# A fast-feedforward tree stage on one core: the leaf mask product over 128 zero-padded rows instead of 16

## What is computed

```python
def _fff(x, node_w, node_b, w1, b1, w2, b2):
    xf = x.reshape(-1, D)
    cur = jnp.zeros((N,), jnp.int32)
    for _ in range(DEPTH):
        score = jnp.einsum('nd,nd->n', xf, node_w[cur]) + node_b[cur]
        cur = 2 * cur + 1 + (score >= 0).astype(jnp.int32)
    sel = jax.nn.one_hot(cur - N_NODES, N_LEAVES, dtype=xf.dtype)
    hidden_all = jax.nn.relu(jnp.einsum('nd,ldh->lnh', xf, w1) + b1[:, None, :])
    hidden = hidden_all * sel.T[:, :, None]
    out = jnp.einsum('lnh,lho->no', hidden, w2) + sel @ b2
    return out.reshape(Bx, Sx, D)
```

## Time and profile before

| | us |
|---|---|
| median of three runs | 1661.69 |
| lowest, highest | 1656.72, 1661.87 |
| the profiled execution, its own time | 1658.01 |
| its span, first to last instruction | 1656.2 |
| TensorE matmul busy in the span | 1468.4 (89%) |
| VectorE, ScalarE, GpSimd busy | 994.2, 652.8, 640.2 |

### The profile page before, as it was taken

The page is one execution under the profiler, slowest core; times in us unless marked ns, Lnnn a source line. Parts: engine busy times, 40 slices in busy tenths (PEclk is TensorE's granted clock), DMA queues, the critical chain, the costliest instruction groups (busy, mean ns, idle before and its releaser), DMA issues. The chain is left out here.

```text
span 1656.2 us, 29794 instructions
## 1 busy us (share of the span) xinstructions
PE 1468.4 (89%) x11472; PEld 1147.0 (69%) x11472; DVE 994.2 (60%) x1896; ACT 652.8 (39%) x1266; POOL 640.2 (39%) x558
## 2 busy tenths in 40 slices
PE   6988877765993899999999999999999994789998
PEld 3645645444893688888888888888888873456676
DVE  4999954476237456666666665666566643464444
ACT  1444432131201455555555555555455431322322
POOL 0000000001002557877767877677876531311100
PEclk9777788867996999999999999999899965899999
DMA  9479700800322666676676675676674531220000
GB/s 357 145 281 323 264 0 1 296 1 0 104 101 88 172 167 153 163 195 164 153 162 155 159 187 150 157 166 148 164 188 101 112 66 51 80 102 0 1 1 26
DMA packets 109296, 219.61 MB, mean 133 GB/s; under 512 B 10871, under 2 KB 83095, under 8 KB 108391
## 3 DMA queue, kind: packets, MB, share of 16 engines
q1 hardware_dynamic: 109163, 217.80, 47.0%
HBM read 132.51 MB, written 6.40 MB: 84 GB/s over the span
## 5 line engine op out<-in xcount | busy, mean ns | idle before, releaser
L1905 DVE TENSOR_REDUCE d_top<-psum 128x1 f32<-128x400 f32 (+2 forms) x512 | 270.4, 570 | 97.6 <-PE psum L1549 90.4
L1449 POOL TENSOR_TENSOR d_ring<-d_ring 128x512 f32<-128x512 f32 x224 | 289.8, 1294 | 77.0 <-ACT d_ring L1734 59.4
L1734 ACT ACTIVATE d_ring<-psum 128x512 f32<-128x512 f32 (+1 forms) x416 | 229.3, 595 | 206.2 <-PE psum L1567 187.2
L1567 PEld LDWEIGHTS psum<-d_queries,d_stack 100*128 100x128 f32 (+1 forms) x1664 | 214.3, 198 | 36.3 <-issue 33.7
L1567 PE MATMUL psum<-d_queries,d_stack 100*128 100x128 f32 (+1 forms) x1664 | 235.4, 286 | 1.2 <-DVE d_queries L1920 0.9
L1549 PE MATMUL psum<-d_stack,d_queries 96*128 96x400 f32 (+1 forms) x512 | 171.6, 393 | 13.4 <-DVE d_top L1905 10.6
L1379 POOL TENSOR_TENSOR d_rowsT<-d_raw,d_rowsT 128x768 fp32r<-128x768 f32 (+2 forms) x62 | 117.9, 1903 | 154.0 <-ACT d_rowsT L1705 154.0
L1534 PE MATMUL psum<-d_wv,d_rowsT 128*128 128x256 f32 (+1 forms) x1248 | 170.4, 286 | 0.0
L1526 PE MATMUL psum<-d_rowsT,d_wk 128*128 128x384 f32 (+2 forms) x768 | 160.3, 358 | 3.6 <-POOL d_rowsT L1379 1.9
L1534 PEld LDWEIGHTS psum<-d_wv,d_rowsT 128*128 128x128 f32 (+1 forms) x1248 | 161.9, 187 | 0.5 <-issue 0.5
L973 POOL TENSOR_TENSOR c_partL<-moe_in,c_partH 128x256 fp32r<-128x256 f32 x8 | 5.5, 730 | 388.5 <-ACT c_partH L1061 388.5
(11 more groups left out here) (393 smaller groups left out, 2303.0 us busy)
## 6 DMA issues: line engine op xcount, KB each, us to landing
d_stack<-d_stage SPq DMA_DIRECT2D x384, 200.2 KB, 4.2
a_cR<-ctx_rows_dram SPq DMA_DIRECT2D x16, 1664.0 KB, 9.5
a_cT<-ctxT_dram SPq DMA_DIRECT2D x16, 1601.0 KB, 14.5
moe_w<-moe_w_dram SPq DMA_DIRECT2D x16, 1024.0 KB, 11.3
d_rowstd<-row_stds_dram SPq DMA_DIRECT2D x16, 801.0 KB, 5.7
d_raw<-ctxT_dram SPq DMA_DIRECT2D x32, 384.0 KB, 5.7
d_raw<-ctxT_dram SPq DMA_DIRECT2D x16, 512.0 KB, 6.3
d_queries<-queries_dram SPq DMA_DIRECT2D x96, 64.0 KB, 2.0
```

The source lines that it names most:

```text
L1449: pool.tensor_tensor(sums[:, 0, m, :], first, ring[:, slot_of(u, m, c), :], ALU.add)\
L1567: last = pe.matmul(ps[0:w, S_BANK + (m + c) % 2, j * P:(j + 1) * P], stack[0:STACKED, m, j, c * P:c * P + w], queries[0:STACKED, m, j, :], ...
L1734: act.activation(ring[0:w, slot_of(u, m, c), :], ps[0:w, S_BANK + (m + c) % 2, :], ACT.Exp)\
L1905: dve.tensor_reduce(top[:, m, v:v + 1], ps[:, M_BANK + v % 2, 0:min(w, S - s0)], X, ALU.max)\
```

## The change

`member`, `leaf_raw` and `leafT` get 128 partitions. `member` becomes three operands, one for each tree, each 128 x 1024 with only that tree's 16 rows other than zero. The matmul of line 2233 so contracts over all 128 partitions for every tree. `path` gets 128 columns, so that `leafT` gets 128 rows, those outside the leaves being zero. On GpSimd a clear of the larger `leaf_raw` (128 x 3072 words) comes second, right after that of `b2_raw`, and SyncE's wait before the six small loads is for both. ScalarE rounds `member` in three instructions of 128 x 1024 where there was one of 80 x 1024, and does so after the last of the four exponentials and before the square roots. The bias matmuls of 16 rows (lines 2244 and 2264) stay.

```diff
-        path = core.tensor(ctx, "f_path", [TREES * NNODE, LEAVES], BF16)
+        path = core.tensor(ctx, "f_path", [TREES * NNODE, P], BF16)
-        leaf_raw = core.tensor(ctx, "f_leaf_raw", [LEAVES, HC * P])
+        leaf_raw = core.tensor(ctx, "f_leaf_raw", [P, TREES, HC * P])
-        leafT = core.tensor(ctx, "f_leafT", [LEAVES, N], F32R)
-        member = core.tensor(ctx, "f_member", [LEAVES, HC, P], F32R)
+        leafT = core.tensor(ctx, "f_leafT", [P, N], F32R)
+        member = core.tensor(ctx, "f_member", [P, TREES, HC * P], F32R)
...
-            sp.wait_ge(sig("f_b2_clear"), 1)
+            sp.wait_ge(sig("f_clear"), 2)
...
-                sp.dma_start(leaf_raw[32 * j:32 * j + rows, :], drams["pg"][0:rows, NN + TREES * D:NN + TREES * D + HC * P])\
+                sp.dma_start(leaf_raw[32 * j:32 * j + rows, j, :], drams["pg"][0:rows, NN + TREES * D:NN + TREES * D + HC * P])\
                   .then_inc(sig("f_leaf_in"), 16)
...
-            pool.memset(b2_raw[:, :], 0.0).then_inc(sig("f_b2_clear"), 1)
+            pool.memset(b2_raw[:, :], 0.0).then_inc(sig("f_clear"), 1)
+            pool.memset(leaf_raw[:, :, :], 0.0).then_inc(sig("f_clear"), 1)
...
-                pe.matmul(ps[0:LEAVES, 2 + c, :], path[:, :], right[:, cols_of(c)], start=True, stop=True)\
+                pe.matmul(ps[:, 2 + c, :], path[:, :], right[:, cols_of(c)], start=True, stop=True)\
                   .then_inc(sig("f_leafT_ps"), 1)
             pe.wait_ge(sig("f_xL"), 2 * KD)
-            pe.wait_ge(sig("f_member"), 1)
+            pe.wait_ge(sig("f_member"), TREES)
...
-                pe.matmul(ps[:, n % 4, :], member[leaves(j), h, :], leafT[leaves(j), cols_of(c)], start=False, stop=True)\
+                pe.matmul(ps[:, n % 4, :], member[:, j, h * P:(h + 1) * P], leafT[:, cols_of(c)], start=False, stop=True)\
                   .then_inc(sig("f_hid_ps"), 1)
...
-            act.activation(member[:, :, :], leaf_raw[:, :].rearrange("p (c n) -> p c n", c=HC), ACT.Copy)\
-               .then_inc(sig("f_member"), 1)
             act.activation(b2[0][:, :], b2_raw[:, :], ACT.Copy).then_inc(sig("f_b2H"), 1)
...
             features(3)
+            for j in range(TREES):
+                act.activation(member[:, j, :], leaf_raw[:, j, :], ACT.Copy).then_inc(sig("f_member"), 1)
...
-                dve.tensor_scalar(leafT[:, cols_of(c)], ps[0:LEAVES, 2 + c, :], 0.5 * DEPTH - 0.5, None, ALU.is_ge).then_inc(sig("f_leafT"), 1)
+                dve.tensor_scalar(leafT[:, cols_of(c)], ps[:, 2 + c, :], 0.5 * DEPTH - 0.5, None, ALU.is_ge).then_inc(sig("f_leafT"), 1)
```

## The result

| | before | after |
|---|---|---|
| median, first measurement (4 runs each) | 1659.2 us | 1636.4 us (1635.03 to 1641.75) |
| ratio | | 0.9875, 95% interval 0.9842 to 0.9908 |
| the profiled execution, its own time | 1658.01 us | 1641.75 us |
| its span | 1656.2 us | 1640.0 us |

In this measurement the change makes the kernel 1.25% faster. The median of 1636.4 us lies 8.6 us under the forecast of 1645 and 3.1 us under the range. The two profiled executions are only 16.3 us apart, close to the 15.6 of the sum. So there are two questions: are the mechanism and its size right, and where do the other microseconds come from.

A forecast was written before the change was run, and what follows sets the result against it. TensorE's instruction stream was taken to bound the rounds. 1658.0 - 16.4 (mask breaks) + 0.75 (stalls) = 1642.4 us, put at a median of 1645 us for the spread between runs; range 1639.5 to 1651.5 us.

The forecast's parts named there:

- the sum: Whole kernel: 1658.0 - 16.4 + 0.75 = 1642.4 us against the profiled execution.
- The bound and the mechanism: Rounds: TensorE's instruction stream bounds them; changing between 16-row and 128-row matmuls costs about 0.39 us in and out.
- The rival of no gain: Masks: the loss belongs to the switch of operands, so a 128-row mask pays it too; 1660 us, chance 0.06.
- that of half a gain: Masks: only one side, into or out of the mask, goes; 8 us off, 1652 us, chance 0.08.
- 42 x 0.39 = 16.4 us: Masks: 42 of 48 stand between full matmuls and lose 0.39 us each, which 128 rows would remove.
- The six places with the bias: Rounds 2, 10, 18, 26, 34, 42: 16-row bias matmuls follow the mask and stay, so no gain counted.
- The stalls: Before rounds 16 and 32: TensorE waits for late weights of trees 1 and 2; two of 0.37 us, 0.75 us back.
- The start of the phase: Clear, loads and rounding ahead of the rounds: longer or later but hidden, nothing charged; at most 0.5 us for clear or rounding.
- the covers: Phase start: 2.7 us clear fills a 2.65 us GpSimd gap; loads hidden by 1.8 us, ScalarE's rounding by 0.4 us.
- The clock: After round 32's eight bias matmuls the clock falls to 0.50, costing some 1.5 us; the fall may go or come elsewhere.
- I leave it as it is: Clock term: the possible 1.5 us gain or loss from falls of the clock was not counted in the forecast.
- Taking that spread in, I put the median after at 1645 us: Whole time: from 1642.4 us, as three runs had a median 3.7 us above the profiled execution and a mean of 1660.1.

The follow-up runs named there:

- the earlier split: Changed kernel with the last piece of the next tree's weights split after round 13 instead of 14; ratio 0.9882, rounds 16 and 32 take 3.02 us.
- the second measurement of the changed kernel: The changed kernel executed again without edit, against the kernel before; median 1638.18 us over six runs, ratio 0.989 (0.9868 to 0.9912).

## Why the prediction was right or wrong

**The bound and the mechanism: right.** TensorE's stream set the time, and each break removed from it came off the time. That the price is for changing between row counts of at most 64 and of 80 or more was shown by the kernel with only the row count undone, and by 64 rows against 80. The rival of no gain falls with the first, that of half a gain with the steps of 0.23 us on both sides of the mask.

**42 x 0.39 = 16.4 us: right, slightly small.** A plain round fell from 3.42 to 3.02 or 3.00, so 0.40 to 0.42; over 42 rounds 16.8 to 17.6. The six places with the bias kept their loss, as stated.

**The stalls: right.** 0.83 us for 0.75, in the rounds named, from the cause named; the earlier split removed them. The second profile of the changed kernel has the same two, 3.42 and 3.45 us against 3.00.

**The start of the phase:** the covers held (clear, loads, rounding), but the loss was 0.2 to 0.9 us where the sum had nothing, and 0.7 us is the usual value over all kernels with the padded operands. `e_gw` began 4.1 us into the phase by the time of the first clear, as before; from 1418 to 1440 us the mean granted clock was 0.69 in the first profile of the changed kernel and 0.77 before, and the first four exponent matmuls took 3.07 us for 2.46. So most of that profile's loss is time at the lower clock. Whether the change brings it about, or the clock stood so by chance, stays open: only two profiles of the kernel before (52.70 and 52.71) stand against twelve of the others.

**The clock: the first step that failed.** "I leave it as it is" valued a term of 1.5 us at nothing. In the rounds, first to last mask, the kernel before needs 171.37 us and the changed one 153.74: 17.6 less. 42 x 0.40 = 16.8, less 0.83 of stalls, makes 16.0; the fall that is gone, 6.78 - 5.29 = 1.5, closes the sum. The row was there, and its neighbour too (one fall in two like stretches); a fall that needs the breaks around it goes when the breaks go (7 of 10 places against 0 of 12). That the stretch of 16-row matmuls would be shortened by one was named as the reason why it might go, and it got no support: with the two masks back at 16 rows alone there was no fall in two places.

**The median: the step that failed by most.** "Taking that spread in, I put the median after at 1645 us" set the sum against 1660.1, the mean of three runs, and gave 2.5 us to both sides for the spread. Further executions of the kernel before have medians of 1656.0 (23), 1655.98 (11), 1656.69 (14) and 1659.19 (12), and single ones go from 1644.82 to 1668.80; the part ahead of the last phase alone moved by 13 us between profiles. Three runs place a median within several microseconds, not 2.5. From 1656.0, the phase's 17.5 us lead to 1638.5; the second measurement of the changed kernel gave 1638.18. Of the 8.6 us missed, 1.9 are the gain (17.5 for 15.6) and 0.5 the rounding up to 1645. The other 6.2 are chance in the two medians, that of the base and that of the four runs after. On the base of 1656.0 they are 4.1 for the base and 2.1 for the four runs; on the median of all 64 executions of the kernel before, 1656.7, they are 3.4 and 2.8. The 1.9 us by which the gain was too small would not have left the range; the 6.2 us did. So the mechanism was right, and the number was lost mainly by trusting medians of three and four runs.

## What to carry to other kernels

When a small matmul stands in a stream of full ones, measure start to start into it and out of it, not its duration: here every such place with up to 64 rows cost 0.39 us for in and out, and zero-padding the contraction over 64 rows (80 sufficed) took it away. Matmuls of few rows side by side cost no more than full ones (0.23 us from start to start). After such a gain look at which handoff had less slack than the rounds got shorter. And when the change is confined to one phase, compare that phase's own length in the profiles; it resolved about 1 us where whole executions of one kernel scattered over 12 us and more.

## What the runs showed of the hardware that I had not expected

- 64 rows cost as much as 16 beside 128-row matmuls (rounds 3.41 us), 80 as little as 128 (2.99), and from 64 to 16 rows costs again (4.53 for 4.35 us).
- TensorE fell to 0.50 of its clock in the middle of a stream without a wait, after eight 16-row matmuls, and only where the rounds around had breaks too (7 of 10 places against 0 of 12 with the same bias). Each cost some 1.5 us. The cause is open.
- Full matmuls of one kernel, 128 rows by 512 columns, follow each other at 0.230 or 0.232 us (a thirteenth of a round of 2.99 or 3.02), and which it is changes between stretches of one execution (3.02, then 2.99, then 3.02 us) and between two executions of the same kernel (the second profile has 3.00, then 3.02 in the same rounds). Over 25 rounds 0.03 us is nearly as much as the stalls. The cause is open.
